# Two graph-attention layers on one core: both normalising passes go from VectorE to ScalarE, in a newly dealt order

## The reference

```python
# layer 0
q, k, v = x @ Wq + bq, x @ Wk + bk, x @ Wv + bv          # split in 8 heads
attn = softmax(where(adj == 0, -inf, q @ k.T / sqrt(32)))
y = (attn @ v) @ Wo + bo + x
x1 = (y - mean(y)) * rsqrt(var(y) + 1e-5) * gamma + beta
# layer 1
q, k, v = x1 @ Wq.T + bq, x1 @ Wk.T + bk, x1 @ Wv.T + bv
pros = softmax(where(adj == 0, -16384, q @ k.T))
z = v
for _ in range(4): z = 0.9 * (pros @ z) + 0.1 * v
y = x1 + z
out = (y - mean(y)) / sqrt(var(y) + 1e-5) * gamma + beta
```

## Time and profile before

| | |
|---|---|
| median of 3 runs | 841.31 us (840.86 to 842.0) |
| profiled execution | 844.29 us, of which span 842.4 us |
| PE busy | 784.4 us, 93% of the span |
| PE weight load busy | 712.4 us, 85% |
| VectorE (DVE) busy | 716.7 us, 85% |
| ScalarE (ACT) busy | 679.4 us, 81% |
| GpSimd (POOL) busy | 554.3 us, 66% |
| HBM traffic | 38 GB/s over the span |

### The profile page before, as it was taken

One profiled execution on the slowest core, in us unless ns is written; L12 is line 12 of the kernel. 1 busy time (PEld: TensorE's weight loads), 2 busy tenths in 40 slices (PEclk: granted clock), 3 DMA queues, 4 the chain that ended last, 5 costly groups with the idle time before them and its releaser, 6 DMA issues. The chain is left out here.

```text
span 842.4 us, 33223 instructions
## 1 busy us (share of the span) xinstructions
PE 784.4 (93%) x11544; PEld 712.4 (85%) x11544; DVE 716.7 (85%) x3409; ACT 679.4 (81%) x2634; POOL 554.3 (66%) x421
## 2 busy tenths in 40 slices
PE   5789999999999999999999999999999999998883
PEld 4678999889889988988899889888988988897661
DVE  4578888899898888999988899898888999988655
ACT  3559988888898888888988888898888888989450
POOL 0236656667676776666777767676777676768566
PEclk9889999999999999999999999999999999999987
DMA  7101100010011111101111110011111101110001
GB/s 221 30 23 46 29 27 15 3 46 20 29 46 46 47 46 47 44 5 46 47 46 47 46 46 26 24 46 46 46 47 46 45 10 40 47 33 28 14 14 63
DMA packets 33219, 34.18 MB, mean 41 GB/s; under 512 B 2336, under 2 KB 28832, under 8 KB 33056
## 3 DMA queue, kind: packets, MB, share of 16 engines
q1 hardware_dynamic: 33056, 32.06, 12.8%
HBM read 23.67 MB, written 8.39 MB: 38 GB/s over the span
## 5 line engine op out<-in xcount | busy, mean ns | idle before, releaser
L590 ACT ACTIVATE ex<-sm,nmax 128x128 f32<-128x128 f32 x1024 | 398.0, 394 | 27.9 <-DVE nmax L738 27.6
L933 POOL TENSOR_TENSOR pr<-ex,rec 128x1024 f32<-128x1024 f32 x128 | 243.4, 1912 | 126.9 <-DVE rec L747 126.6
L738 DVE CUSTOM_DVE_ANT_0 sm<-psS,mask 128x128 f32<-128x128 f32 x1024 | 229.5, 284 | 6.8 <-PE psS L362 6.5
L590 ACT ACTIVATION_READ_ACCUMULATOR ex<-sm,nmax 128x1 f32 x1024 | 197.3, 193 | 0.0
L372 PE MATMUL psF<-ident,pr 128*128 128x128 f32 x1024 | 150.0, 280 | 5.5 <-issue 3.0
L599 ACT ACTIVATE pT<-psF 128x512 f32<-128x512 f32 x224 | 126.3, 593 | 30.6 <-PE psF L372 26.4
L372 PEld LDWEIGHTS psF<-ident,pr 128*128 128x128 f32 x1024 | 116.5, 143 | 17.4 <-issue 11.6
L313 PE MATMUL psF<-xh,w_hi 128*128 128x256 f32 x512 | 115.3, 307 | 14.2 <-DVE w_lo L677 7.5
L380 PE MATMUL psF<-pT,z 128*32 128x128 f32 x3072 | 110.5, 276 | 3.6 <-DVE z L840 2.7
L313 PE MATMUL psF<-xh,w_lo 128*128 128x256 f32 x512 | 104.2, 286 | 0.0
L313 PE MATMUL psF<-xl,w_hi 128*128 128x256 f32 x512 | 104.1, 285 | 0.0
(11 more groups left out here) (67 smaller groups left out, 1496.2 us busy)
## 6 DMA issues: line engine op xcount, KB each, us to landing
xt_in<-in_x_t SPq DMA_DIRECT2D x32, 256.0 KB, 3.5
x_in<-in_x SPq DMA_DIRECT2D x32, 256.0 KB, 3.1
out<-o_t SPq DMA_DIRECT2D x32, 256.0 KB, 2.2
adj_in<-in_adj SPq DMA_DIRECT2D x32, 128.0 KB, 2.9
w_raw<-in_w SPq DMA_DIRECT2D x7, 256.0 KB, 4.6
row<-in_rows SPq DMA_DIRECT2D x1, 768.0 KB, 6.5
ident<-in_ident SPq DMA_DIRECT2D x1, 64.0 KB, 3.8
col<-in_cols SPq DMA_DIRECT2D x1, 7.0 KB, 3.9
```

The source lines that it names most:

```text
L590: e = nc.scalar.activation(ex[l][:, b, h, :], sm[l][:, b, h, :], ACT.Exp, scale=-1.0, bias=nmax[l][:, b, h:h + 1], accum_out=tot[l][:, b, ...
L738: last = nc.vector.tensor_tensor_reduce(sm[l][:, b, h, :], psS[:, o:o + N], mask[p.parity][:, b, :], -1.0, BIG, ALU.add, ALU.min, nmax[l][ ...
L933: nc.gpsimd.tensor_tensor(pr[l][:, b, :, :], ex[l][:, b, :, :], rec[l][:, b, :].unsqueeze(2).broadcast_to([128, H, N]), ALU.mult).then_inc ...
```

## The change

- `normalise(l, b, p)` becomes a ScalarE activation per graph, `Identity(rstd × y + mterm)` with scale and bias by row, for both layers; `mean_term` on VectorE makes mterm = −mean × rstd (128x2). The semaphores `xn_done` and `out_normed` are split by graph.
- For the last two pairs (30 and 31) the final normalisation, scale and shift are `finish` on VectorE, two `scalar_tensor_tensor` per graph, and each graph is stored by a DMA of its own; GpSimd's two passes fall away there.
- `save_x1h` moves from ScalarE to VectorE. `save_q` and `save_k` on VectorE become one instruction of 128x512 in place of two of 128x256. ScalarE takes layer 0's keys, VectorE layer 1's. VectorE does three `save_hop` a step in place of four, ScalarE five in place of four.
- All PSUM bank assignments and the orders in every engine's `step` are new. `scores(0, t)` is now in step t, not in the next; the folds are made in step 0, not in step 1; `save_y`, `statistics(0)` and `aggregate(0)` end VectorE's step.

```diff
+            def normalise(l, b, p):
+                if p.real and not (l and p.last_two):
+                    act.wait_ge(mt_s[l].sem, mt_s[l].at(p))
...
+                    nc.scalar.activation(dst[:, b, :], y[:, b, :], ACT.Identity, bias=mterm[l][:, b:b + 1],
+                                         scale=rstd[l][:, b:b + 1]).then_inc(done.sem, 1)
...
+            def finish(b, p):
+                if p.last_two:
...
+                    nc.vector.scalar_tensor_tensor(out=o_t[p.parity][:, b, :], in0=y1[p.parity][:, b, :],
+                                                   scalar=mv[1][:, b, 0:1], in1=row[:, GA1, :],
+                                                   op0=ALU.subtract, op1=ALU.mult).then_inc(scaled_s[b], 1)
+                    dve.wait_ge(scaled_s[b], n)
+                    nc.vector.scalar_tensor_tensor(out=o_t[p.parity][:, b, :], in0=o_t[p.parity][:, b, :],
+                                                   scalar=rstd[1][:, b:b + 1], in1=row[:, BE1, :],
+                                                   op0=ALU.mult, op1=ALU.add).then_inc(end_s[b], 1)
+
+            def mean_term(l, p):
+                if p.real and not (l and p.last_two):
...
+                    nc.vector.scalar_tensor_tensor(out=mterm[l][:, :], in0=mv[l][:, :, 0], scalar=-1.0, in1=rstd[l][:, :],
+                                                   op0=ALU.mult, op1=ALU.mult).then_inc(mt_s[l].sem, 1)
```

More of the change, by code:

```diff
@@ L138, in two_layers @@
         rstd = [sb(f"rstd{l}", [128, 2]) for l in range(2)]
+        mterm = [sb(f"mterm{l}", [128, 2]) for l in range(2)]
         oh = sb("oh", [128, 2 * C, N], F32R)
@@ L194, in two_layers @@
         ve_s = [count(f"var_eps{l}_done") for l in range(2)]
-        xn_s = count("xn_done")
-        on_s = count("out_normed")
+        xn_s = [count(f"xn{b}_done") for b in range(2)]
+        on_s = [count(f"out{b}_normed") for b in range(2)]
         z_s = over_jb("hop_saved")
@@ L203, in two_layers @@
         rstd_s = [count(f"rstd{l}_done") for l in range(2)]
+        mt_s = [count(f"mean_term{l}") for l in range(2)]
         z0_s = count("z0s_done")
@@ L227, in two_layers @@
         fold_s = sem("folds_saved")
+        scaled_s = [sem(f"last_scaled{b}") for b in range(2)]
+        end_s = [sem(f"last_out{b}") for b in range(2)]
         block = ctx.enter_context(nc.Block())
@@ L450, in step @@
-                free((v_s[0], t - 1), (hT_s[1][1], t - 5))
-                turn_probs(1, 0, 1, t - 4)
[L452 to L460, removed]
+                free((ol_s, t - 2), (pT_s[0][1][0], t - 2), (hT_s[1][1], t - 5))
@@ L461, in step @@
+                values(1, 0, t - 3)
+                values(1, 1, t - 3)
+                free((pT_s[1][1][0], t - 4))
+                hop(0, 1, t - 4)
                 free((pT_s[1][0][1], t - 4))
                 hop(0, 0, t - 4)
[L463 to L467, removed]
@@ L476, in step @@
+                if t.is_(1):
+                    pe.wait_ge(fold_s, 3)
                 keys(0, 0, t)
[L477 to L480, removed]
+                free((hT_s[0][1], t - 4), (pT_s[1][1][0], t - 4), (y_s, t - 2))
+                turn_x1(t - 2)
                 keys(0, 1, t)
-                free((v_s[1], t - 3), (hT_s[0][0], t - 4), (pT_s[1][0][1], t - 4), (v_s[0], t - 1))
@@ L532, in step @@
+                hop(2, 0, t - 4)
+                free((mx[1][0][0], t - 2), (mx[0][0][1], t - 1))
+                scores(0, t)
+                if t.is_(0):
+                    pe.wait_ge(q_s[0].sem, q_s[0].at(P0))
+                    pe.wait_ge(v_s[0].sem, v_s[0].at(P0))
                     folds()
-                free((pT_s[0][1][0], t - 1), (hT_s[2][0], t - 4))
-                hop(2, 1, t - 4)
             run(step, 0, PAIRS + 5)
@@ L988, in scale_out @@
             def scale_out(p):
-                if p.real:
-                    pool.wait_ge(on_s.sem, on_s.at(p))
+                if p.real and not p.last_two:
+                    for b in range(2):
+                        pool.wait_ge(on_s[b].sem, on_s[b].at(p))
                     nc.gpsimd.tensor_tensor(o_t[p.parity][:, :, :], o_t[p.parity][:, :, :], both(row[:, GA1:GA1 + 1, :]),
```

354 lines of the change are left out of this document (198 added, 156 removed).

## The result

| | before | after |
|---|---|---|
| median, same chip | 841.65 us (840.86 to 844.94, 4 runs) | 832.94 us (829.82 to 835.39, 4 runs) |
| profiled execution, span | 844.29, 842.4 us | 834.3, 832.4 us |
| PE, DVE, ACT, POOL busy | 93, 85, 81, 66% | 94, 80, 88, 66% |

The ratio is 0.9887, 95% interval [0.9842, 0.9933]. The change gains, but 8.7 us and not 26.9: the forecast of 814.5 and its range of 804 to 830 are missed. The runs of after spread over 5.6 us.

The account below looks back on a forecast made before the run. PE, 23.82 us busy of a 24.28 us step, was taken as the bound. Steady −17.0, step before −1.9, four earlier steps −1, folds −1, end −6 gave −26.9 off 841.31: 814.5 us, range 804 to 830.

Parts of the forecast that it names:

- ol was late through o_t's pair: Steady step: POOL's pr holds DVE's o_t pair, 2.27 us against xn's 0.73; late ol costs PE 0.62.
- The bound of 23.35: Steady step: lower bound in us of the forecast 23.6, if the other small waits go too; upper bound 24.1.
- The price of `mean_term`: DVE's steady step: two mean_term on 128x2 at about 0.2 us each, by L812's 204 ns; 0.40 in all.
- the w_lo of 2.20: DVE instruction at 24.84 with two SBUF inputs: 2.20 us where its size is 0.68, while POOL executed pr.
- rival 2: POOL holds mean_term, in layer 0 delaying normalisations, turn_x1 and ACT's queue: step 24.8, time 848 us, slower; chance 0.05.
- My hand order: One new step walked, PE never waiting: all margins positive, 0.4 to 1.1 us, so near 23.5 possible.
- Rival 1: ACT, at 22.8 of 23.5, brings pT late to attend: step 23.9 to 24.1, time 823 to 828; chance 0.20.
- The begin: Up to the sixth ol: step before the steady ones −1.9, four before −1, moved folds −1 (between −4 and +4).
- The end: After the steady steps: −6 us, between −3 and −9, from the last o_t pairs and the last stores.
- my −3.5: Last pair: four DVE instructions end at 836.2 where POOL's scale and shift ended at 839.77: −3.5 us.
- Caught are 1.5 us each: Step 32 and the two after it have a held o_t pair; freeing them, on the end's chain in part: −3.
- my +0.5: End: the other last pair's four DVE instructions stand ahead of the last hop work: +0.5 us.

Follow-up runs that it names:

- single: The changed kernel with mean_term as two one-column instructions, rstd as scalar by row in place of a second tensor: 820.59 us, ratio 0.9734 to the kernel before.
- x_first: The changed kernel with load_x(t + 1) issued ahead of store(t - 6) on SP's queue: 840.03 us, ratio 0.9962 to the kernel before.
- x_single: The changed kernel with both edits, load_x ahead of the store and mean_term as one-column instructions: 821.01 us, ratio 0.9738 to the kernel before.
- act_late: single with two more ScalarE activations a step into an unread tile, ahead of the xh cast where no xn waits: 821.95 us, ratio 0.9747 to before.
- single_folds: single with PE's folds back in step 1 behind attend(1, 0), save_fold and add_bias(0) moved with them: 819.72 us, ratio 0.9729 to the kernel before.
- hop_first: single_folds with, in step 33 alone, save_hop(2, 1) between layer 1's masks instead of behind them: 819.65 us, ratio 0.9719 to the kernel before.
- hop_free: hop_first with PE's free wait ahead of scores(0, t) made only where t is a real pair: 818.52 us, ratio 0.9710 to the kernel before.
- ot_back: The changed kernel with o_t's two normalisations back on VectorE at the place of layer 1's mean_term: 870.22 us, ratio 1.0333 to the kernel before.

## Why the prediction was wrong

**What bounds the kernel, and what a step can be: right.** PE is the bound, ol was late through o_t's pair, and without stalls a step is 23.5: single's is 23.41, PE busy throughout. The bound of 23.35 was never reached. DVE's busy time was forecast too low (19.2, single's is 19.76), which cost nothing.

**The price of `mean_term`: the step that failed.** I wrote "two mean_term on 128x2, about 0.2 each by L812's 204". L812 reads one tensor; this one reads two, both in SBUF. It measured 0.703 in the mean and 0.15 to 1.85 single. The document's own had the right neighbour, the w_lo of 2.20 beside pr, and rival 2 was built on it. With mean_term at 0.33 a pair (single) the kernel takes 820.6, inside my range and 6 above the forecast: of the miss of 18.4 us, 12 to 14 are this term (12.4 by the medians, 14.2 by the profiled spans).

It acts in all three parts of the span. Steady: after's mean step is 592.75/25 = 23.71, single's 23.42, so 7.2 us. Begin: single's sixth ol is at 150.68, 3.9 us before after's; 0.7 of that stands already at the first ol, ahead of any mean_term. Behind it layer 0's pair is held by POOL's xb too (1.07 at 46.05, xb until 47.10), and PE's `turn_x1` waits:

```profile
48.34 1.09 PE L421 MATMUL psF<-ident,xn 128*128 128x128 f32 x4 [1.29 <-ACT xn L636]
71.40 1.09 PE L421 MATMUL psF<-ident,xn 128*128 128x128 f32 x4 [1.95 <-ACT xn L636]
```

These four transposes take 0.60 in a steady step and 1.09 here: the granted clock of both stretches is 0.50 (1.2 of 2.4 GHz). At the first it had fallen before, in an idle time of 4.02 that ended at 45.44, and single's first takes 1.08 as well. At the second it fell in the wait of 1.95; in single that wait is 1.22, the clock stays at 1.00, and they take 0.63. The mean clock from first to second ol is 0.85 in single against 0.79 in after, from second to third 1.00 against 0.92. End: mterm is 1.85 in step 32, and that step takes 23.75 against single's 21.87.

**Rival 2, "POOL catches mean_term instead": the mechanism was right, its place and its chance wrong.** I looked only at layer 0, where a late mterm keeps `turn_x1` waiting, and found POOL's operation there short, rightly: restart_term (z0s) stretches it to 0.51 in a steady step and nothing waits. It is layer 1's, 6 us later in DVE's order, that meets pr (or zf), with `add_hop(3, 0)` and PE behind it. My hand order had margins for ol, z, xn and x1l, and none for this `turn_hop`; it is reached when mean_term takes 0.65. And the price I gave, 848, took every step as the worst one; by x_first, where every step is held for 1.27, it is 840.
The Trainium skill (SBUF — State Buffer, Who interferes with whom) says that VectorE with two SBUF inputs and a GpSimd instruction that reads SBUF contend, and that the later one is blocked for the whole of the other's instruction; by that rule the cost was foreseeable. The traces agree, 546.64 against 546.63 above.

**An overlooked queue.** I walked one step for four engines and left SP's out. There `load_x(t + 1)` stands behind `store(t - 6)`; x_in lands 0.5 to 2.5 us late for POOL, which alone costs nothing (x_single) but shifts POOL against DVE. No forecast that takes POOL's places from a hand order could have told 0.73 from 1.59.

**Rival 1, ScalarE late (0.20): not what happened.** ACT is busy 22.7 as forecast, but with 23.19 in act_late the step is still 23.41. What I had right is that its margins are small: xn, forecast 0.9, has 0.4.

**The begin: −3.9 forecast, +5.3 measured; +1.4 in single.** Apart from the holding, two things. The folds delay the first ol from 34.70 to 38.23, of which by the second between 0.1 and 1.3 are left (single_folds, hop_first, hop_free): inside my −4 to +4, on the other side. And the intervals are redistributed: second to third ol is 20.19 in single against 18.65 before, since xn now comes by way of POOL's pow, DVE's mterm and ACT with a longer chain and nothing else for PE to do (`turn_x1` waits 1.22 there, at 69.05, and did not wait in the kernel before); the last interval, from the fifth ol to the sixth, is 23.41 against 25.5: −2.1, of which I had counted 1.9.

**The end: −6 forecast, −1.1 measured; −4.2 in single.** The last store did come sooner, as I worked out. From the last pow on it is 832.4 − 828.3 = 4.1 us in place of 842.4 − 834.4 = 8.0, −3.9 against my −3.5:

```profile
828.33 0.48 DVE L869 SCALAR_TENSOR_TENSOR o_t<-y,mv,row 128x256 f32<-128x256 f32 x1 [0.81 <-POOL rstd L1005]
...
829.77 0.48 DVE L873 SCALAR_TENSOR_TENSOR o_t<-o_t,rstd,row 128x256 f32<-128x256 f32 x1
```

The −3 for "Caught are 1.5 us each" did not come, even in single (−0.3 between the 31st ol and the last pow, my +0.5 counted in it). One wait there is found, PE's 2.4 us for DVE's masks in step 33; hop_free, which takes most of it away, is 1.0 shorter there. The rest of the 3 stays open.

By single's numbers the terms are −21.4 steady (forecast −17.0), +1.4 begin (−3.9) and −4.2 end (−6): the steady part was mis-sized in my favour, the edges against me.

## What to carry to other kernels

Price a tiny instruction by its operands and by what runs beside it, not by its size: two tensors in SBUF on VectorE can cost as much as GpSimd's longest instruction. The repair here was to work one column at a time, with one value read as a scalar by row, which turned a gain of 9 us into one of 23; on 128x256 an instruction with its values by row was held all the same. And when a step is walked, walk every queue, SP's too, and note a margin for each reader of each buffer; then test whether an engine at 97% is loaded or only late, by putting the same work at another place.

## What the runs showed of the hardware

- VectorE on 128x2 with two SBUF tensors took 0.15 to 1.85 us, and in 59 of after's 62 it ended within 0.03 us of a GpSimd instruction; with one tensor and a scalar by row on one column it took 0.206 us, never held in 124 (single). On 128x256 the normalisation with one tensor and both values by row was held (before 2.27, ot_back 2.11 a pair, against 0.73).
- It goes the other way as well. In single, pow on 128x2 started at 507.29, in the middle of DVE's xl cast of two SBUF inputs (507.11 to 507.80), and took 1.07 us. All 30 that started inside that cast took 1.07 or 1.08, the other 34 took 0.69 to 0.72:

```profile
507.29 1.07 POOL L1007 TENSOR_TENSOR rstd<-ve,mhalf 128x2 f32<-128x2 f32 x1 [1.08 <-DVE ve L848]
...
512.94 0.71 POOL L1007 TENSOR_TENSOR rstd<-ve,mhalf 128x2 f32<-128x2 f32 x1
```

- An activation with scale and bias by row on 128x256 took 591 to 610 ns in the mean, 0.49 from start to start, and none of them was held by GpSimd.
- ScalarE busy 23.19 us of a step of 23.41 did not lengthen it (act_late).
